# Feed-forward layer after attention: the maximum between the taps, VectorE's results in a PSUM bank, the second norm over slots a group ahead, and w2 loaded in parts

## The chip, the cores and the metric

The program runs on the 8 cores of one Trainium2 chip. Each core takes one sequence of 2048 tokens of width 1024 and works alone; nothing is exchanged. The metric is the device time of the slowest core, in microseconds. The engines are named as in the profile: PE (TensorE), DVE (VectorE), ACT (ScalarE), POOL (GpSimd) and SP (SyncE, which here only starts transfers).

## The reference, cut to what matters

```python
x = x + attention(layernorm(x))            # 16 heads of 64, causal
x = x + ffn(layernorm(x))

def ffn(x):                                # w1 [4096,1024], w2 [1024,4096]
    h = bit_linear(x, w1)                  # x rounded to 8 bits per token, w to -1, 0, 1
    h = depthwise_conv1d(h over tokens, conv_w [4096,1,3], padding 1) + conv_b
    h = silu(h)
    return bit_linear(h, w2)               # h rounded with max|h| over the token's 4096 channels

def act_quant(x):
    scale = 127 / clip(max(|x|, last axis), 1e-5)
    return clip(round(x * scale), -128, 127) / scale
```

The second rounding needs, for each token, the largest absolute value over all 4096 hidden channels. That maximum ("the maximum" below) is what ties the two products together.

## The kernel before, in words

The first half is attention: eight head pairs of 40 slots each (`hp`, `s`), a program order written out by hand for every engine. In the last head pair DVE also takes the statistics of the second norm for the first token tiles, rounds the last pieces of the weights (`weight_step`) and ends with `normalize_ctx`. The sum x1 is spilled to HBM (`x1scr`), and its SBUF space is reused by the feed-forward's buffers, `w2T` among them.

The feed-forward works on 8 groups `G` of 256 tokens. A group has 8 slots `b`, one for each 512 hidden channels (a "quad" `q = 8*G + b`). In every slot:

- PE: `first(q)` makes four blocks `psM[0..3]` of 128 channels by 258 tokens, 8 matmuls each. A block can be overwritten once ACT has read it (`a_tB`) and DVE has read it (`v_tap`). From G = 2 on `second(G-2, b)` follows, 16 matmuls of 512 columns of the second product.
- ACT: `taps(q)` reads each of the four blocks twice, for the right tap with the bias (into `hs`) and the left tap (into `tb`); then `silu(q-1)`, for which POOL must have added `tb` to `hs`.
- DVE: `taps(q)` adds the middle tap from each of the four blocks; `widen_max(q-1)` takes the maximum over the 4 x 128 channels of the quad before, out of what `silu` wrote: a reduction of 128 x 1024 and, but for a group's first quad, a `tensor_tensor` that joins it with the running maximum `amf`.
- POOL: `add_taps(q)`, four additions, then for the group before `scale_h`, four multiplications per quad by the token's scale.

For the group before, DVE rounds the scaled quads into `hqa` or `hqb` (`round_h`, by the table `ROUNDED`; POOL's quads by `SCALED`); `hs` is a ring of 12 quads, so ACT's `taps(q)` waits until quad q-12 is rounded. `token_scale`, `turn_max` and `spread_scale` turn the maximum into the scale row `srow`. `add_out` finishes a half of 128 output rows.

The second norm of the tokens of the next group but one runs beside it: DVE takes `stats` of two token tiles in slots b = 0 and 1 of group G, `spread` and `factors` follow in b = 1 and 2, ACT's `rstd2` (Ln, Exp) in b = 2 and `round_xq` in b = 3 and 4, POOL's `place_xqs`, PE's `transpose_xq` and ACT's `place_xqT` after that. ACT keeps one function table at a time; Ln and Exp, and then Silu, load one each.

SP's queue is in order too. The weight blocks of the first product (`load_w1(q)`, 512 KB) are loaded two slots ahead; the whole of w2 (4 x 1 MB) is loaded in one go in G = 0, b = 5.

Of the kernel before, what the change touches and what calls it, by code (L numbers as in the profile page):

```python
# [16 lines left out]
D = 1024  # L17
# [10 lines left out]
NP = 8  # L28
# [25 lines left out]
def build_program():  # L54
# [23 lines left out]
    with es:  # L78
# [20 lines left out]
        d_x1t = [sem("d_x1t0"), sem("d_x1t1"), sem("d_x1t2")]  # L99
# [133 lines left out]
        x1t = sb("x1t", [128, 3 * D], F32, esB)  # L233
        amx = sb("amx", [128, GRP], F32, esB)
# [4 lines left out]
        psTb = ps("psTb", [128, 1024], BF16, esB)  # L239
        psNb = ps("psNb", [128, 512], F32, esB)  # L240
        psM = [ps(f"psM{i}", [128, 512], F32, esB) for i in range(4)]
# [51 lines left out]
        def tokens(e, st):  # L293
            if st < 5:
                e.wait_ge(g_x1, 4 * (NP - 1) + st // 4 + 1)
                return x1_tile(st)
            e.wait_ge(d_x1t[st % 3], 16 * ((st - 5) // 3 + 1))
            return x1t[:, (st % 3) * D:(st % 3 + 1) * D]

        def lcol(i, k, n):  # L300

            at = 48 * (i % 2) + 3 * k
            return lnc[:, at:at + n]

# [14 lines left out]
        ROUNDED = {3: (0, 1), 4: (2,), 5: (3, 4), 6: (5,), 7: (6,)}  # L319

# [15 lines left out]
        def _(e):  # L336
# [71 lines left out]
            def load_x1t(st):  # L408
                if st >= 8:
                    e.wait_ge(a_xqf, st - 2)  # L410
                e.dma_start(out=x1t[:, (st % 3) * D:(st % 3 + 1) * D],
                            in_=x1scr[128 * st:128 * (st + 1), :]
                            ).then_inc(d_x1t[st % 3], 16)
# [16 lines left out]
            for st in (5, 6, 7):  # L430
                load_x1t(st)
# [3 lines left out]
            for G in range(NGRP + 2):  # L435
                for b in range(8):
                    q = 8 * G + b + 2
                    if 3 <= q < 8 * NGRP:
                        load_w1(q)
                    if b == 1 and G >= 3:  # L440
# [7 lines left out]
                    if b in (6, 7) and 8 <= 2 * G + b - 1 < NT:  # L448
                        load_x1t(2 * G + b - 1)
# [13 lines left out]
        def _(e):  # L463
# [158 lines left out]
            for G in range(NGRP + 1):  # L622
                for b in range(8):
                    if G < NGRP:
                        add_taps(8 * G + b)
                    if b == 4 and G < 7:
                        place_xqs(2 * G + 3)
                    if b == 5 and G < 6:
# [6 lines left out]
        def _(e):  # L635
# [129 lines left out]
            def transpose_xq(st):  # L765
                e.wait_ge(g_xqs, st + 1)
                if st == 0:
# [100 lines left out]
            def turn_max(g):  # L868
                at = (g % 2) * GRP
                e.wait_ge(v_max, 8 * (g + 1))  # L870
                if g >= 1:
                    e.wait_ge(a_srow, g)
                e.transpose(psNb[:, 0:128], amf[:, at:at + 128], idf[:])
# [652 lines left out]
```

## Time and profile before

| what | value |
|---|---|
| time, median of 3 runs | 1073.35 us (1069.76 to 1102.9) |
| time of the profiled execution | 1075.98 us |
| its span on the slowest core (core 6) | 1074.4 us |
| spans of the other cores | 1056.5 to 1072.5 us |
| busy share of the span | PE 83%, DVE 75%, ACT 65%, POOL 64% |
| first matmul of the feed-forward | 522.11 us |
| DMA, mean over the span | 155 GB/s |

The profile is of one execution on one core. A busy share is an average over stages with different limits, so each stage is read for itself.

### The profile page before, as it was taken

How to read it: one execution, taken by the hardware profiler on the slowest of the kernel's cores; microseconds unless marked ns; L12 is line 12 of the kernel's file. 1: busy time of each engine (PE TensorE's matmuls, PEld its weight loads, DVE VectorE, ACT ScalarE, POOL GpSimd, SP SyncE). 2: the span in 40 equal slices, each digit the busy share in tenths (PEclk: the TensorE clock that was granted, in tenths of full speed). 3: DMA queues.
4: the chain of work that ended last, by engine and by line, in shares of the span. 5: the costliest groups of instructions: out<-in, count | busy, mean ns of one | idle time of the engine just before them, and what ended most of it. 6: DMA issues, size and time to landing. Idle time of an engine off the chain costs nothing.

```text
span 1074.4 us, 23923 instructions; the slowest of 8 cores (1056.5 to 1074.4 us)
## 1 busy us (share of the span) xinstructions
PE 895.0 (83%) x7282; PEld 539.3 (50%) x7340; DVE 806.9 (75%) x1293; ACT 698.2 (65%) x1116; POOL 682.7 (64%) x912
## 2 busy tenths in 40 slices
PE   2999989897957778866676578999989899999898
PEld 1454545454524444433554455666656565666443
DVE  2674776777778888977377979898897989888631
ACT  3553888797827676868686866767677676766200
POOL 2211755646655768565454795959879597979590
PEclk9999999999979999967888989999999999999899
DMA  8910777666665766684744221423314233332112
GB/s 265 328 62 1 197 209 236 244 201 223 206 211 173 217 196 202 211 296 161 261 172 182 71 87 59 158 99 132 125 66 151 99 121 116 116 105 96 40 41 77
DMA packets 38749, 166.89 MB, mean 155 GB/s; under 512 B 4833, under 2 KB 4962, under 8 KB 29922
## 3 DMA queue, kind: packets, MB, share of 16 engines
q1 hardware_dynamic: 34210, 148.59, 41.8%
q0 software_dynamic: 4416, 16.78, 4.4%
q8 instruction: 63, 1.03, 0.4%
q14 instruction: 60, 0.49, 0.1%
HBM read 140.18 MB, written 25.17 MB: 154 GB/s over the span
## 4 chain that ended last, share of the span: by engine, by line
PE 42%; DVE 19%; issue 12%; POOL 9%; ACT 8%; DMA 7%; DVEq 1%; SPq 1%; POOLq 0%; ACTq 0%
PE psM L843 9%; PE psO L861 9%; POOL hs L618 6%; PE psQK L680 6%; PE psV L660 5%; PE psS L738 5%; PE psPV L757 5%; DVE hs L1367 3%; ACT PT L999 3%; DVE t1s L1208 3%; DVE amx L1386 3%; ACT hs L1044 2%; DMA wvst<-wv 2%; DMA t1scr<-t8s 2%; ACT tb L1048 2%
## 5 line engine op out<-in xcount | busy, mean ns | idle before, releaser
L999 ACT ACTIVATE PT<-psS,nbias 128x1024 bf16<-128x1024 f32 (+1 forms) x320 | 297.5, 985 | 89.2 <-PE psS L738 85.5
L843 PE MATMUL psM<-xqT,w1b 128*128 128x258 bf16 x2048 | 249.7, 283 | 44.3 <-DVE hs L1367 35.6
L609 POOL TENSOR_TENSOR hs<-hs,tb 128x256 f32<-128x256 f32 x256 | 200.1, 811 | 106.7 <-DVE hs L1367 106.1
L843 PEld LDWEIGHTS psM<-xqT,w1b 128*128 128x128 fp8e4 x2048 | 203.9, 101 | 91.5 <-issue 54.1
L1044 ACT ACTIVATE hs<-psM,convb_s,convw_s 128x256 f32<-128x256 f32 x256 | 146.3, 572 | 99.5 <-PE psM L843 88.0
L618 POOL TENSOR_TENSOR hs<-hs,srow 128x256 f32<-128x256 f32 x256 | 190.0, 775 | 12.0 <-ACT srow L1062 12.0
L680 PE MATMUL psQK<-ln1T,wqkb 128*128 128x512 bf16 x430 | 116.6, 391 | 23.3 <-DVE qkO L1135 7.4
L757 PE MATMUL psPV<-vaug,PT 128*128 128x65 bf16 x2176 | 116.9, 200 | 19.7 <-DVE ctx L1189 10.7
L757 PEld LDWEIGHTS psPV<-vaug,PT 128*128 128x128 bf16 x2176 | 93.1, 101 | 80.1 <-issue 59.4
L1367 DVE SCALAR_TENSOR_TENSOR hs<-psM,convw_s,hs 128x256 f32<-128x256 f32 x256 | 108.5, 473 | 20.1 <-ACT tb L1048 19.4
L1048 ACT ACTIVATE tb<-psM,convw_s 128x256 f32<-128x256 f32 x256 | 121.7, 475 | 0.0
L494 POOL TENSOR_TENSOR PT<-PT,mask_s 128x256 bf16<-128x256 bf16 x128 | 94.0, 750 | 40.9 <-ACT PT L999 39.3
L861 PE MATMUL psO<-w2T,hqa 128*128 128x512 fp8e4 x512 | 117.3, 385 | 0.0
L861 PE MATMUL psO<-w2T,hqb 128*128 128x512 fp8e4 x512 | 114.7, 379 | 2.4 <-DVE hqb L1419 1.7
L1386 DVE TENSOR_REDUCE amx<-hs 128x256 f32<-128x1024 f32 x56 | 108.4, 1936 | 4.6 <-ACT hs L1055 4.6
L505 POOL TENSOR_TENSOR x<-x,ctx 128x128 f32<-128x128 f32 x128 | 70.3, 581 | 56.7 <-DVE ctx L1189 56.5
L861 PEld LDWEIGHTS psO<-w2T,hqa 128*128 128x128 f16 x512 | 50.7, 99 | 57.2 <-issue 3.2
L485 POOL TENSOR_TENSOR sqb<-qkE 128x512 bf16<-128x512 bf16 x32 | 36.6, 1143 | 67.2 <-DVE qkE L1135 64.9
L861 PEld LDWEIGHTS psO<-w2T,hqb 128*128 128x128 f16 x512 | 49.9, 98 | 58.6 <-issue 3.3
L738 PE MATMUL psS<-qkO 64*128 64x512 bf16 (+3 forms) x320 | 62.4, 388 | 19.0 <-ACT PT L999 18.2
L1199 DVE TENSOR_REDUCE smalls<-wbuf 128x1 f32<-128x2048 f32 x32 | 72.8, 2274 | 4.9 <-DMA wbuf<-w2p 3.1
L1055 ACT ACTIVATE hs<-hs 128x1024 f32<-128x1024 f32 x64 | 68.2, 1066 | 12.3 <-POOL hs L609 12.3
(125 smaller groups left out, 1132.8 us busy)
## 6 DMA issues: line engine op xcount, KB each, us to landing
wbuf<-w1q SPq DMA_DIRECT2D x32, 1024.0 KB, 6.4
wbuf<-w2p SPq DMA_DIRECT2D x32, 1024.0 KB, 5.9
w1b<-t1scr SPq DMA_DIRECT2D x64, 512.0 KB, 3.5
x<-x SPq DMA_DIRECT2D x16, 512.0 KB, 15.0
wqkst<-wqk POOLq DMA_DIRECT2D x16, 512.0 KB, 6.7
x1scr<-x POOLq DMA_DIRECT2D x4, 2048.0 KB, 10.1
x1g<-x1scr SPq DMA_DIRECT2D x16, 512.0 KB, 4.4
out<-x1g SPq DMA_DIRECT2D x16, 512.0 KB, 2.6
```

Source lines behind the costliest of these rows:

```text
L609: e.tensor_tensor(hs_quad(q)[:, part], hs_quad(q)[:, part], tb_quad(q)[:, part], ALU.add).then_inc(g_add, 1)
L618: inst = e.tensor_tensor(part, part, srow[:, at:at + GRP], ALU.mult)
L680: inst = e.matmul(bank[:], wqkb[:, at:at + 128], ln1T[:, x0:x0 + 512], start=(kc == 0), stop=(kc == 7))
L738: inst = e.matmul(bP[:, 512 * h + 128 * j:512 * (h + 1)], qk[64 * h:64 * (h + 1), k0:k0 + 128], qk[64 * h:64 * (h + 1), q0:q0 + n], start= ...
L757: inst = e.matmul(psPV[:, 512 * h + VW * m:512 * h + VW * (m + 1)], pt_unit(u)[:, p0:p0 + 128], vaug[:, v0:v0 + VW], start=(kc == 0 and m ...
L843: inst = e.matmul(psM[j][:, 0:GRP + 2], w1b[:, at:at + 128], xqT[:, x0:x0 + GRP + 2], start=(kc == 0), stop=(kc == 7))
L861: inst = e.matmul(psO[n][:], hq_of(g)[:, at:at + 128], w2T[:, D * kc + 512 * n: D * kc + 512 * (n + 1)], start=(kc == 0), stop=(kc == 31))
L999: e.activation(out=pt_unit(u).rearrange("p (h w) -> p h w", w=512)[:, :, 128 * j:512], in_=psS[u % 2][:].rearrange("p (h w) -> p h w", w=512)[
L1044: e.activation(out=hs_quad(q)[:, GRP * j:GRP * (j + 1)], in_=psM[j][:, 2:GRP + 2], func=AF.Identity, scale=convw[:, 3 * hh + 2:3 * hh + 3] ...
L1048: e.activation(out=tb_quad(q)[:, GRP * j:GRP * (j + 1)], in_=psM[j][:, 0:GRP], func=AF.Identity, scale=convw[:, 3 * hh:3 * hh + 1]).then_i ...
L1367: e.scalar_tensor_tensor(sl, psM[j][:, 1:GRP + 1], convw[:, 3 * hh + 1:3 * hh + 2], sl, ALU.mult, ALU.add).then_inc(v_tap, 1)
L1386: done(e.tensor_reduce(amx[:], rows, AX.X, ALU.max, apply_absolute_value=True))
```

## The change

The order of work in the feed-forward is rewritten in these places:

- The maximum of the quad before stands between the second and the third middle tap of a slot, and all else of DVE's slot behind the fourth.
- A PSUM bank, free since `psTb` and `psNb` share one, becomes `psD`. It holds the first part of the maximum, a copy of the identity, and most short results of the second norm and the token scale.
- The statistics of a token tile are split (`moments2`, `largest`, `smallest`) and spread over the slots b = 4 to 7 of the group before and b = 0 and 1; those of batch 1 (tiles 3 and 4) move into the last head pair, slots 29 to 36, with `rstd2(1)` on ACT in slot 33. In G = 0 `round_xq` and what follows come two slots earlier (`TAKEN`).
- w2 is loaded in four parts, one behind each `load_w1` of q = 5 to 8. A fourth buffer for x1 tiles is added.

```diff
-            def taps(q):
-                for j in range(4):
+            def taps(q, js):
+                for j in js:
...
-                    done(e.tensor_reduce(amx[:], rows, AX.X, ALU.max,
+                    done(e.tensor_reduce(psD[:, 0:GRP], rows, AX.X, ALU.max,
                                          apply_absolute_value=True))
                     settled()
-                    e.tensor_tensor(top, top, amx[:], ALU.max
+                    e.tensor_tensor(top, psD[:, 0:GRP], top, ALU.max
                                     ).then_inc(v_max, 1)
...
             for G in range(NGRP + 2):
                 for b in range(8):
                     if G < NGRP:
-                        taps(8 * G + b)
+                        taps(8 * G + b, (0, 1))
+                    if 1 <= 8 * G + b <= 8 * NGRP:
+                        widen_max(8 * G + b - 1)
+                    if G < NGRP:
+                        taps(8 * G + b, (2, 3))
                     if b == 0 and 2 <= G <= NGRP + 1:
                         round_h(8 * (G - 2) + 7)
-                    if 1 <= G <= NGRP:
-                        for k in ROUNDED.get(b, ()):
-                            round_h(8 * (G - 1) + k)
+                    if b == 1 and 1 <= G <= NGRP:
+                        token_scale(G - 1)
                     if b == 0 and G >= 3:
                         add_out(4 * (G - 3) + 3)
                     if b in (2, 4, 6) and G >= 2:
                         add_out(4 * (G - 2) + b // 2 - 1)
-                    if 1 <= 8 * G + b <= 8 * NGRP:
-                        widen_max(8 * G + b - 1)
...
+                    if G < 6:
+
+                        if b == 4:
+                            moments2(G + 2, 0)
+                        if b == 5:
+                            largest(G + 2, 0)
+                        if b == 6:
+                            smallest(G + 2, 0)
+                        if b == 7 and G < 5:
+                            moments2(G + 2, 1)
...
+                    if 1 <= G <= NGRP:
+                        for k in ROUNDED.get(b, ()):
+                            round_h(8 * (G - 1) + k)
...
+                    if s == 33:
+                        rstd2(1)
...
-                    if b == 2 and G < 7:
+                    if b == 1 and 1 <= G < 7:
                         rstd2(G + 1)
...
+                    if s in (29, 31):
+                        moments2(1, (s - 29) // 2)
+                        largest(1, (s - 29) // 2)
+                        smallest(1, (s - 29) // 2)
+                    if s == 31:
+                        variance(1)
+                    if s == 36:
+                        factors(1)
...
+                    if 3 <= q - 2 <= 6:
+                        load_w2(q - 5)
...
-                    if G == 0 and b == 5:
-
-                        e.wait_ge(a_xqf, 5)
-                        for q4 in range(4):
-                            e.dma_start(
-                                out=w2T[:, 8 * q4 * D:8 * (q4 + 1) * D],
-                                in_=t2scr[:, 8 * q4 * D:8 * (q4 + 1) * D]
-                            ).then_inc(d_w2, 16)
```

DVE, group 1, the slots b = 3 and the start of b = 4, with what each row waits for (`hs<-psM` are middle taps, the reduction and the TENSOR_TENSOR behind it the maximum of the quad before, `hqb<-hs` the rounding). Before:

```order
L1367 SCALAR_TENSOR_TENSOR hs<-psM,convw_s,hs 128x256 [waits a_tB] x4
L1419 TENSOR_SCALAR hqb<-hs 128x1024 [waits g_mul] x2
L1386 TENSOR_REDUCE amx<-hs 128x256 [waits a_silu,v_max]
L1389 TENSOR_TENSOR amf<-amf,amx 128x256 [waits v_own]
L1367 SCALAR_TENSOR_TENSOR hs<-psM,convw_s,hs 128x256 [waits a_tB] x4
```

The same place now:

```order
L1410 SCALAR_TENSOR_TENSOR hs<-psM,convw_s,hs 128x256 [waits a_tB] x2
L1429 TENSOR_REDUCE psD<-hs 128x256 [waits a_silu,v_max]
L1432 TENSOR_TENSOR amf<-psD,amf 128x256 [waits v_own]
L1410 SCALAR_TENSOR_TENSOR hs<-psM,convw_s,hs 128x256 [waits a_tB] x2
L1463 TENSOR_SCALAR hqb<-hs 128x1024 [waits g_mul] x2
L1410 SCALAR_TENSOR_TENSOR hs<-psM,convw_s,hs 128x256 [waits a_tB] x2
```

The wait for `a_silu` stood behind all four taps and the two roundings; now it stands ahead of the third tap, and the roundings stand behind the maximum.

DVE, the end of the last head pair (`t1s` and `t8s` are the last weight step, `recb` and `ctx` the last `normalize_ctx`). Before:

```order
L1208 TENSOR_SCALAR t1s<-wbuf,smalls 128x2048
L1211 TENSOR_SCALAR t1s<-t1s 128x2048
L1214 TENSOR_SCALAR t8s<-t1s 128x2048
L1181 RECIPROCAL recb<-psPV 128x8
L1189 TENSOR_TENSOR ctx<-psPV,recb 128x4x64 x2
```

Now, ahead of the same step and behind it (the second tile's statistics and the first of the factors; the first tile's stand above):

```order
L1267 BN_STATS bn6b<-x 128x6
L1268 BN_STATS bn6b<-x 128x6
L1271 BN_AGGR lnc<-bn6b 128x2
L1275 TENSOR_REDUCE psD<-x 128x1
L1280 TENSOR_REDUCE psD<-x 128x1
L1296 TENSOR_SCALAR lnc<-lnc 128x2
L1231 TENSOR_SCALAR t1s<-wbuf,smalls 128x2048
L1234 TENSOR_SCALAR t1s<-t1s 128x2048
L1237 TENSOR_SCALAR t8s<-t1s 128x2048
L1303 TENSOR_TENSOR psD<-psD,lnc 128x2
```

The statistics of two tiles come ahead of the last weight step and the factors between it and `normalize_ctx`.

SP, the loads of G = 0. Before:

```order
L411 DMA x1t<-x1scr 128x1024 x3
L418 DMA x1g<-x1scr 128x1024 x2
L387 DMA w1b<-t1scr 128x4096 x5
L454 DMA w2T<-t2scr 128x8192 x4
L387 DMA w1b<-t1scr 128x4096 x10
```

Now:

```order
L400 DMA w1b<-t1scr 128x4096 x3
L432 DMA w2T<-t2scr 128x8192
L400 DMA w1b<-t1scr 128x4096
L432 DMA w2T<-t2scr 128x8192
L400 DMA w1b<-t1scr 128x4096
L432 DMA w2T<-t2scr 128x8192
L400 DMA w1b<-t1scr 128x4096
L432 DMA w2T<-t2scr 128x8192
L400 DMA w1b<-t1scr 128x4096 x7
```

The block of four parts ahead of the load for q = 8 is taken apart, one part behind each of four blocks of w1.

## Rows read from the trace of the kernel before

**Rows 1.** Busy time by stretch, from one group's last silu to the next

```profile
core 6: us, PE busy (x) PEld busy (x) DVE busy (x) ACT busy (x) POOL busy (x), PEclk, DMA share, GB/s
533.68:579.32 45.64, 32.90 (x250) 25.91 (x249) 33.84 (x60) 37.80 (x71) 23.30 (x33) 0.85 0.53 202
579.32:639.25 59.93, 36.93 (x274) 28.49 (x273) 51.41 (x79) 43.35 (x83) 46.45 (x61) 0.86 0.24 80
639.25:702.79 63.54, 58.39 (x406) 38.34 (x404) 56.30 (x87) 43.66 (x82) 51.71 (x68) 1.00 0.30 100
...
830.31:893.33 63.02, 58.50 (x406) 38.40 (x404) 55.63 (x87) 43.66 (x82) 50.68 (x67) 1.00 0.32 110
893.33:952.31 58.98, 57.41 (x397) 38.25 (x396) 53.27 (x86) 41.39 (x80) 51.00 (x68) 1.00 0.31 108
952.31:1005.23 52.92, 52.92 (x358) 34.83 (x356) 44.39 (x63) 32.94 (x67) 47.04 (x63) 1.00 0.26 91
```

**Rows 2.** Timeline, ACT and DVE in quad 5's slot: start, duration, what, idle before

```profile
559.93 0.64 ACT L1044 ACTIVATE hs<-psM,convb_s,convw_s 128x256 f32<-128x256 f32 x1
...
560.74 1.14 ACT L1055 ACTIVATE hs<-hs 128x1024 f32<-128x1024 f32 x1
...
562.05 1.96 DVE L1386 TENSOR_REDUCE amx<-hs 128x256 f32<-128x1024 f32 x1 [0.53 <-ACT hs L1055]
564.11 0.43 DVE L1389 TENSOR_TENSOR amf<-amf,amx 128x256 f32<-128x256 f32 x1
564.45 1.40 DVE L1367 SCALAR_TENSOR_TENSOR hs<-psM,convw_s,hs 128x256 f32<-128x256 f32 x3
```

**Rows 3.** Timeline, PE and ACT: from a tap to matmuls, from matmuls to ACT

```profile
565.08 3.68 PE L843 MATMUL psM<-xqT,w1b 128*128 128x258 bf16 x32 [0.32 <-DVE hs L1367]
...
596.27 3.68 PE L843 MATMUL psM<-xqT,w1b 128*128 128x258 bf16 x32 [3.12 <-DVE hs L1367]
...
597.41 0.56 ACT L1044 ACTIVATE hs<-psM,convb_s,convw_s 128x256 f32<-128x256 f32 x1 [0.24 <-PE psM L843]
...
600.05 0.56 ACT L1044 ACTIVATE hs<-psM,convb_s,convw_s 128x256 f32<-128x256 f32 x1
```

**Rows 4.** Source lines L1389 and L1367: duration ns min/median/max

```profile
L1389 DVE TENSOR_TENSOR amf<-amf,amx x56: 424/822/996, 544.5 to 1011.8; 128x256 f32<-128x256 f32 x56
...
L1367 DVE SCALAR_TENSOR_TENSOR hs<-psM,convw_s,hs x256: 465/472/485, 525.1 to 1002.0; 128x256 f32<-128x256 f32 x128
```

**Rows 5.** Timeline: PE after an idle stretch in group 1

```profile
587.05 5.67 PE L843 MATMUL psM<-xqT,w1b 128*128 128x258 bf16 x32 [3.49 <-DVE hs L1367]
```

**Rows 6.** Busy time and granted clock of that stretch, columns as in rows 1

```profile
587.00:590.00 3.00, 2.95 (x14) 2.09 (x15) 3.00 (x5) 0.93 (x2) 2.78 (x4) 0.50 0.02 5
```

**Rows 7.** Timeline, ACT: a table load ahead of silu

```profile
790.86 1.28 ACT L1055 ACT_TABLE_LOAD   x1
```

**Rows 8.** Timeline, slot b = 4 of group 4: roundings, and ACT waiting for them

```profile
796.21 2.21 DVE L1419 TENSOR_SCALAR hqb<-hs 128x1024 f16<-128x1024 f32 x2
...
797.49 0.56 ACT L1044 ACTIVATE hs<-psM,convb_s,convw_s 128x256 f32<-128x256 f32 x1 [1.32 <-DVE hqb L1419]
```

**Rows 9.** Timeline, POOL around two scaled quads (b = 4 and 5)

```profile
805.16 1.19 POOL L524 TENSOR_SCALAR xqs<-xqf,lnc 128x1024 bf16<-128x1024 f16 x1
...
812.43 3.23 POOL L609 TENSOR_TENSOR hs<-hs,tb 128x256 f32<-128x256 f32 x4
```

**Rows 10.** Timeline, PE's wait for the last maximum

```profile
1012.51 0.45 PE L873 MATMUL psNb<-idf_s,amf 128*128 128x128 f32 x1 [4.74 <-DVE amf L1389]
```

**Rows 11.** Timeline, PE at the first slot of group 1

```profile
573.05 8.87 PE L843 MATMUL psM<-xqT,w1b 128*128 128x258 bf16 x64 [4.29 <-DMA w1b<-t1scr]
```

**Rows 12.** Timeline, DVE at the end of attention: two tiles' statistics, the last wait

```profile
477.19 0.69 DVE L1246 BATCH_NORM_STATS2 bn6b<-x 128x6 f32<-128x512 f32 x1 [1.33 <-POOL x L505]
...
480.77 0.68 DVE L1246 BATCH_NORM_STATS2 bn6b<-x 128x6 f32<-128x512 f32 x1
...
518.01 0.21 DVE L1181 RECIPROCAL recb<-psPV 128x8 f32<-128x8 f32 x1 [8.79 <-PE psPV L757]
```

More of the change, by code:

```diff
@@ L98, in build_program @@
         d_w1 = [sem("d_w1_0"), sem("d_w1_1"), sem("d_w1_2")]
-        d_x1t = [sem("d_x1t0"), sem("d_x1t1"), sem("d_x1t2")]
+        d_x1t = [sem(f"d_x1t{i}") for i in range(4)]
         d_x1g = [sem("d_x1g0"), sem("d_x1g1")]
@@ L408, in load_x1t, with load_w2 @@
             def load_x1t(st):
[L409 to L411 removed]
+                if st >= 9:
+                    e.wait_ge(a_xqf, st - 3)
+                e.dma_start(out=x1t[:, (st % 4) * D:(st % 4 + 1) * D],
                             in_=x1scr[128 * st:128 * (st + 1), :]
[L413 removed]
+                            ).then_inc(d_x1t[st % 4], 16)
+            def load_w2(q4):
+                if q4 == 0:
+                    e.wait_ge(a_xqf, 5)
+                e.dma_start(out=w2T[:, 8 * q4 * D:8 * (q4 + 1) * D],
+                            in_=t2scr[:, 8 * q4 * D:8 * (q4 + 1) * D]
+                            ).then_inc(d_w2, 16)
             def load_x1g(u):
@@ L429, in _ @@
             e.wait_ge(d_x1s[1], 16)
-            for st in (5, 6, 7):
+            e.wait_ge(d_x1s[2], 16)
+            for st in range(5, 9):
                 load_x1t(st)
@@ L1262, in var_of, with variance @@
                     "p (n k) -> p n k", k=2)[:, :, 1]
-            def spread(i):
+            def variance(i):
                 n = len(batch(i))
@@ L1280, in factors @@
                 settled()
+                e.tensor_tensor(pcol(i, 12, n), pcol(i, 2, n), mean_of(i, n),
+                                ALU.subtract)
+                done(e.tensor_tensor(lcol(i, 13, n), pcol(i, 3, n),
+                                     mean_of(i, n), ALU.add))
+                settled()
+                done(e.tensor_tensor(pcol(i, 7, n), pcol(i, 12, n),
+                                     lcol(i, 13, n), ALU.max))
+                settled()
                 e.wait_ge(a_rstd2, i + 1)
-                done(e.tensor_tensor(lcol(i, 14, n), lcol(i, 7, n),
+                done(e.tensor_tensor(pcol(i, 14, n), pcol(i, 7, n),
@@ L1345, in _ @@
                     place_bias(c - 1)
-                if hp == NP - 1 and s in (9, 12, 16):
-                    stats(0, s // 4 - 2)
-                if hp == NP - 1 and s == 16:
-                    spread(0)
-                if hp == NP - 1 and s == 21:
-                    factors(0)
+                if hp == NP - 1:
+                    if s in (12, 14, 17):
+                        moments2(0, (12, 14, 17).index(s))
+                        largest(0, (12, 14, 17).index(s))
+                        smallest(0, (12, 14, 17).index(s))
+                    if s == 17:
+                        variance(0)
+                    if s == 21:
+                        factors(0)
+                    if s in (29, 31):
[6 more added lines that the diff above has]
+                        factors(1)
                 if slot in STEPS:
@@ L1432, in add_out @@
                                        ALU.mult, ALU.add).then_inc(v_epi2, 1)
+            done(e.tensor_copy(psD[:, 256:384], idf[:]))
+            settled()
             for G in range(NGRP + 2):
```

117 lines of the change are left out of this document (62 added, 55 removed).

## The prediction

> **What bounds the kernel now.** I read the busy time by stretch first, cut at the start of each group's last silu, since silu is where the hidden quads pass from one engine to the next. The feed-forward has three regimes [rows 1]. In the first two stretches (groups 0 and 1, 45.64 and 59.93 us) PE runs only the first product: it is busy 33 and 37 us, at a granted clock of 0.85, and ACT, DVE and POOL set the pace. The next four, of which the first and the last are shown, take 254.1 us together, 63.5 each: PE is busy for 58.4, DVE for 56.3, POOL for 51.7. The sixth takes 58.98, and in the seventh (52.92, seven slots and a short one) PE is busy all the time. PE needs about 7.0 us a slot when nothing holds it. So there are some 5 us to win in each of four groups, more in groups 0 and 1, and nothing in the last. A slot of DVE is so full before because the statistics sit in b = 0 and 1.
>
> Then I looked for who waits for whom within a slot: timelines of the slots where an engine stands idle and the releaser is named [rows 2, 3]. A small latency means nothing in a sum of busy times, but it counts where the order closes a ring.
>
> **The ring that the change closes.** Before, DVE took all four taps of quad q and then the maximum of q-1; a late silu was worth a slot of slack. Now the third and the fourth tap stand behind the maximum of q-1, and that waits for silu(q-1), which ACT runs behind its own taps of q. The third tap frees `psM[2]`, PE can then make block 2 of q+1, ACT must read blocks 2 and 3, and only then comes silu(q). One turn advances by exactly one slot, and it has no slack in it. Its length, step by step:
> - silu starts to reduction starts: 562.05 - 560.74 = 1.31 us; reduction to the joining TENSOR_TENSOR: 564.11 - 562.05 = 2.06 [rows 2].
> - TENSOR_TENSOR to tap: 564.45 - 564.11 = 0.34 [rows 2]. The new one reads one operand from PSUM, as the tap does; so it should take the tap's 0.47, not 0.43, and the step 0.38.
> - tap to matmuls: 565.08 - 564.45 = 0.63 [rows 2, 3].
> - matmuls to ACT's read: 597.41 - 596.27 = 1.14; one block on ACT: (600.05 - 597.41) / 3 = 0.88 [rows 3].
> - the last block's read to silu: 560.74 - 559.93 = 0.81 [rows 2].
>
> The sum is 7.21 us a slot. That is a floor for every slot that has taps, whatever is taken off DVE's load. It is just above PE's 7.0, so it costs little where PE was the bound, but where PE has only the first product a slot could be shorter than that.
>
> **What lies on the ring beside it**, in each of groups 1 to 6:
> - The table load ahead of silu, 1.28 us [rows 7], once a group, since Ln and Exp stand between two silus. 1.3. The one ahead of Ln fits into ACT's wait for PE, as do `round_xq` and `place_xqT`.
> - The roundings. In b = 3 they now come behind the maximum and the fourth tap, and ACT's taps of b = 4 need the first of them (ring of 12 quads). Counted from silu: 3.75 to the third tap, two taps of 0.46 (three take 1.40) [rows 2], and ACT starts 797.49 - 796.21 = 1.28 after the first rounding [rows 8]: 5.95. Four blocks and silu follow, 3 x 0.88 + 0.81, which makes 9.40 against 7.21: 2.2.
> - POOL in b = 4. It can add blocks 2 and 3 only behind the late taps: 4.22 + two additions of 0.81 = 5.9. Then `place_xqs` and two scaled quads, 812.43 - 805.16 = 7.3, and four additions of the next quad, 3.23 [rows 9]: done at 16.4, where silu is due at 14.4. 2.0.
> - 0.5 for PE's transposes and POOL's next slot, an estimate from the same rows.
>
> Together 6.0, so a group takes 8 x 7.21 + 6.0 = 63.7. Against the stretches [rows 1]:
> - group 0: 7 x 7.21 = 50.5 against 45.64: +4.8. Here the statistics are gone, the batch 1 table loads too, and it is still longer.
> - group 1: 63.7 against 59.93: +3.8.
> - four groups: 254.8 against 254.1: +0.7.
> - the sixth stretch: 63.7 against 58.98: +4.7.
> - the seventh: seven slots, 5.6 us to the last silu (it follows the two late taps and POOL's two additions, with no taps of ACT ahead), the roundings' 2.2 and POOL's 0.8 (no `place_xqs` there): 59.1 against 52.92: +6.2.
>
> That is +20.2.
>
> **PE's clock in groups 0 and 1.** There PE has 3.7 us of work a slot, so in a turn of 7.2 it stands idle for 3.5 us, and what it does next is the ring's own step. After 3.12 us idle the trace has four blocks in 3.68 us [rows 3]; after 3.49 us in 5.67 us, at a granted clock of 0.50, the 1.2 GHz level [rows 5, 6]. [...] The two blocks in the ring at half clock cost 1.8 us more; the whole difference of these rows is 2.0. Over 15 slots that is 27, less some 4 in group 1, where PE is waited for less because the roundings and POOL are late: 23. Idle stretches will not all be equal, the first two blocks of the next quad may come apart from the others, and neighbouring rows lie on both sides: I take two thirds, +16, and keep 0 and 23 as ends. The Trainium skill (TensorE: Matmul & The Clock Gate, section on HAM oscillation) describes this for another kernel: idle gaps between bursts of matmuls put every burst that follows at half clock, not some of them. By it all 15 slots would pay, which is a rival below.
>
> **The other parts.**
> - Results in PSUM. The joining TENSOR_TENSOR takes 0.42 us at best and 0.82 in the median [rows 4], the tap with one operand in PSUM never over 0.49. So about 0.35 goes in seven of eight slots, 2.5 us a group of DVE's time, and some of the tiny operations of the norm with it. All of it falls into DVE's wait for silu, so I cost it at nothing. If the new form still took 0.82, the ring would be 0.35 longer, some 17 us over 49 slots; if PE rather than the ring bounds, it is a gain (the rival).
> - DVE's other work has 7.21 less the maximum and the taps, 7.21 - 2.44 - 1.84 = 2.9 us a slot; DVE's 56.3 us a group [rows 1] less eight taps and maxima leave about 2.4. It fits, if spread; a slot that overflows lengthens the ring directly, 0 to 1 us a group.
> - w2 in parts. PE waited 4.29 us for the block of w1 behind it [rows 11]. With one 1 MB part ahead of each block and two slots of 7.2 us in hand it is hidden; were it not, at most these 4.3 us come back. The gain lies inside group 0, which the ring already gives a length.
> - End of attention. Two tiles' statistics, 480.77 - 477.19 = 3.6 us each, go ahead of the last weight step and the factors behind it. DVE then waited 8.79 us for PE [rows 12], which hides them. ACT gets `rstd2(1)` with a wait for DVE in the middle of its exponents: +1.2, between 0.5 and 3. Behind DVE's later last step stands SP's last store of w2, and the feed-forward's start behind that; if the cover is too short it costs up to 2 more.
> - The tail. The last maximum no longer waits for POOL and a rounding: 1.31 + 2.06 + 0.6 = 4.0 after the last silu (1005.23 [rows 1]) in place of 1012.51 - 1005.23 = 7.3 [rows 10]: -3.3. POOL's scaling of the last group follows from that directly.
>
> **The sum.** 20.2 + 16 + 1.2 - 3.3 = +34 us on the profiled execution's 1075.98 (span 1074.4). That execution lies 2.6 over the median of three, so I put the difference on the median: 1073.35 + 34 = 1107 us.
>
> **The rivals.**
> 1. Clock low in every slot of groups 0 and 1 (the page's rule, above): +23 instead of +16, 1114 us, up to 1122 with the upper ends of the small terms. For it: rows 5. Against it: the 3.12 us idle that stayed fast.
> 2. The ring binds, PE stays at full clock: 20.2 + 1.2 - 3.3 = +18, 1091 us; 1080 if the roundings and POOL also cost half. For it: rows 3, and the 3.5 us are near that row too.
> 3. The change does nothing to speak of: what the ring costs in groups 0, 6 and 7 comes back from DVE's lighter load, because DVE's wait for a full slot was longer than I see. 1073, between 1063 and 1080.
> 4. Faster: the ring does not bind, DVE's load does. Then the four groups come down to the 59.0 of the sixth stretch (-18), group 0 to ACT's 37.8 busy (-7.8), group 1 to DVE's 51.4 (-8.5) [rows 1], and the tail gives 3.3: -36, 1037 us. It decides from a turn of under 7.0 us. Against it: every step is a measured start to start, and the smallest alternative rows shorten it by 0.2 at most. For it: in four long stretches DVE and PE both are near full, and that is what spreading the statistics helps.
>
> **Chances.** Forecast (1098 to 1112) 0.40, rival 1 0.14, rival 2 0.24, rival 3 0.10, rival 4 0.12. A measurement of this kernel tells 2% from no change, so slower begins at 1095: the forecast, rival 1 and the upper fifth of rival 2 give 0.58; rival 3, the rest of rival 2 and a little of rival 4 within 2%, 0.31; faster 0.11. The range leaves out rival 4 and the top of rival 1: 1066 to 1122 us.
>
> **What would show it.** In the new profile: silus 7.2 us apart in the second half with DVE idle ahead of each reduction, released by silu, and PE idle ahead of its first-product matmuls, released by the tap; groups 0 and 1 at 50 to 75 us each with a granted clock near 0.75; the TENSOR_TENSOR at 0.47; the table load only in ACT's rows of b = 1; no wait for a transfer at the start of group 1; the last maximum 4 us behind the last silu. I am wrong if DVE has no idle time ahead of the maximum, or silus in group 0 lie closer than 7 us.

## The result, and the profile after

The changed kernel takes 1100.88 us (median of 5 runs, 1098.02 to 1141.68) against 1073.35: a ratio of 1.025, 95% interval 1.021 to 1.029. The top of the range is a run in which half of the cores ran at a lower clock, and every ratio here leaves such runs out. It is slower by 27.5 us, and the forecast was 1107, 34 slower. The profiled execution has a span of 1096.4 us on its slowest core (core 3) against 1074.4 (core 6), 22.0 more.

Busy time by stretch of the changed kernel, cut at each group's last silu as in [rows 1]; the sixth and seventh stretch stand fourth and fifth here, and the last row runs to the end of the program:

```profile
528.30:583.94 55.64, 34.30 (x230) 25.21 (x231) 32.11 (x49) 35.34 (x67) 21.63 (x30) 0.80 0.53 191
583.94:647.42 63.48, 39.68 (x278) 29.09 (x277) 48.62 (x82) 43.23 (x83) 46.71 (x63) 0.86 0.24 84
...
712.63:775.61 62.98, 58.34 (x406) 38.33 (x405) 52.41 (x89) 43.63 (x83) 50.06 (x67) 1.00 0.35 118
...
903.80:971.72 67.92, 60.78 (x398) 39.02 (x397) 49.57 (x78) 41.55 (x80) 48.09 (x66) 0.95 0.29 94
971.72:1031.25 59.53, 56.12 (x368) 35.42 (x366) 43.06 (x63) 33.06 (x67) 46.91 (x64) 1.00 0.24 81
1031.25:1096.40 65.15, 54.62 (x244) 24.27 (x244) 18.84 (x26) 1.44 (x2) 27.65 (x36) 0.97 0.17 65
```

Against [rows 1]: group 0 +10.0, group 1 +3.6, the four middle stretches +2.3 together (65.21, 62.98, 65.21, 62.98), the sixth +8.9, the seventh +6.6, the stretch behind the last silu -4.0 (65.15, against 1074.4 - 1005.23 = 69.17). Silu 0 came 5.4 us earlier, at 528.30 against 533.68. That adds up to the 22.0 us between the spans.

One core of one execution has its own accidents, so here is the same division for all eight cores of the two profiled executions (us, changed less before):

| stretch | forecast | slowest cores | mean of eight cores |
|---|---|---|---|
| up to silu 0 | +1.2 | -5.4 | +0.9 |
| group 0 | +4.8 | +10.0 | +9.0 |
| group 1 | +3.8 | +3.6 | +5.0 |
| PE's clock in groups 0 and 1 | +16 | in the two rows above | in the two rows above |
| four middle stretches | +0.7 | +2.3 | +2.9 |
| sixth | +4.7 | +8.9 | +5.1 |
| seventh | +6.2 | +6.6 | +6.7 |
| behind the last silu | -3.3 | -4.0 | -3.5 |
| together | +34 | +22.0 | +26.3 |

The point to see is DVE: in the four middle stretches it is busy for 53.4 us in the mean in place of 56.1, 2.7 us less, and the stretches are no shorter (64.1 us for 63.5). Work went away and waiting took its place.

Who waits, in the feed-forward of the changed kernel (us in total, times, longest):

```profile
ACT hs L1067 <- PE psM L862: 113.8, 72, 3.5
DVE psD L1429 <- ACT hs L1078: 88.9, 44, 4.7
...
PE psM L862 <- DVE hs L1410: 68.5, 44, 4.2
...
ACT hs L1067 <- DVE hqb L1463: 15.5, 3, 7.9
ACT hs L1078 <- POOL hs L625: 14.4, 7, 5.2
ACT hs L1067 <- DVE hqa L1463: 12.4, 3, 4.8
...
PE psM L862 <- DMA w1b<-t1scr: 3.0, 1, 3.0
```

The first three close a circle: DVE's maximum waits for silu, PE's first product for DVE's tap, ACT's read for PE. In the kernel before, PE waited 35.6 us for the tap and the reduction 4.6 us for silu. One turn of that circle, timeline of quads 27 and 28:

```profile
744.85 1.10 ACT L1078 ACTIVATE hs<-hs 128x1024 f32<-128x1024 f32 x1
...
746.11 1.95 DVE L1429 TENSOR_REDUCE psD<-hs 128x256 f32<-128x1024 f32 x1 [2.17 <-ACT hs L1078]
...
748.17 0.42 DVE L1432 TENSOR_TENSOR amf<-psD,amf 128x256 f32<-128x256 f32 x1
...
748.51 0.87 DVE L1410 SCALAR_TENSOR_TENSOR hs<-psM,convw_s,hs 128x256 f32<-128x256 f32 x2
...
749.13 1.92 PE L862 MATMUL psM<-xqT,w1b 128*128 128x258 bf16 x16 [1.75 <-DVE hs L1410]
...
750.27 0.56 ACT L1067 ACTIVATE hs<-psM,convb_s,convw_s 128x256 f32<-128x256 f32 x1 [1.56 <-PE psM L862]
...
751.15 0.57 ACT L1067 ACTIVATE hs<-psM,convb_s,convw_s 128x256 f32<-128x256 f32 x1
...
751.97 1.05 ACT L1078 ACTIVATE hs<-hs 128x1024 f32<-128x1024 f32 x1
```

The steps are 1.26, 2.06, 0.34, 0.62, 1.14, 0.88 and 0.82: 7.12 us. From silu to silu the undisturbed slots of the whole second half take 7.06 to 7.13 us. Each middle group has three longer ones: 8.61 with the table load, 9.47 where ACT waits for the roundings (798.35 to 807.82, and alike in other groups), and 9.45 where POOL is late.

One thing the prediction did not have. Timeline of DVE, POOL and ACT in group 6 of the changed kernel:

```profile
930.64 2.77 POOL L625 TENSOR_TENSOR hs<-hs,tb 128x256 f32<-128x256 f32 x4
...
931.47 5.83 DVE L1463 TENSOR_SCALAR hqb<-hs 128x1024 f16<-128x1024 f32 x2
...
933.37 2.77 POOL L634 TENSOR_TENSOR hs<-hs,srow 128x256 f32<-128x256 f32 x4
...
936.90 0.56 ACT L1067 ACTIVATE hs<-psM,convb_s,convw_s 128x256 f32<-128x256 f32 x1 [7.91 <-DVE hqb L1463]
```

Two roundings, 2.2 us together in [rows 8], take 5.83 here: the first stands open over POOL's eight operations in a row, which end at 936.14. ACT, which needs the buffer, loses 4 us more than in other groups (a slot of 13.6 us). On core 0 of the same execution this slot is 9.5 us, so it is a matter of how the engines happen to lie to one another.

### The profile page after: what moved, and what is told of

Read it like the earlier page. It is cut to its first block, busy times and chain, and to the rows that moved or that the text cites. A ratio compares the mean times of both kernels' runs of the same rounds, so it can differ in the third digit from the quotient of the medians.

```text
span 1096.4 us, 24048 instructions; the slowest of 8 cores (1083.4 to 1096.4 us)
## 1 busy us (share of the span) xinstructions
PE 913.0 (83%) x7340; PEld 539.9 (49%) x7340; DVE 783.5 (71%) x1302; ACT 695.9 (63%) x1114; POOL 677.8 (62%) x912
## 4 chain that ended last, share of the span: by engine, by line
PE 45%; DVE 15%; issue 11%; POOL 11%; ACT 10%; DMA 6%; DVEq 1%; SPq 0%; POOLq 0%; ACTq 0%
PE psM L862 11%; PE psO L880 9%; PE psQK L696 7%; DVE psD L1429 5%; PE psV L676 5%; PE psS L754 5%; PE psPV L773 5%; POOL hs L634 5%; ACT hs L1078 3%; ACT PT L1020 3%; DVE hs L1410 2%; POOL hs L625 2%; ACT tb L1071 2%; DMA wvst<-wv 2%; DMA x1scr<-x 2%
## 5 line engine op out<-in xcount | busy, mean ns | idle before, releaser
L862 PE MATMUL psM<-xqT,w1b 128*128 128x258 bf16 x2048 | 260.1, 285 | 75.8 <-DVE hs L1410 68.5
L625 POOL TENSOR_TENSOR hs<-hs,tb 128x256 f32<-128x256 f32 x256 | 195.4, 786 | 146.4 <-DVE hs L1410 139.2
L634 POOL TENSOR_TENSOR hs<-hs,srow 128x256 f32<-128x256 f32 x256 | 186.3, 759 | 8.2 <-ACT srow L1085 8.2
L1429 DVE TENSOR_REDUCE psD<-hs 128x256 f32<-128x1024 f32 x56 | 108.7, 1941 | 89.2 <-ACT hs L1078 88.9
L696 PE MATMUL psQK<-ln1T,wqkb 128*128 128x512 bf16 x480 | 130.1, 397 | 6.7 <-DVE qkO L1158 5.2
L1410 DVE SCALAR_TENSOR_TENSOR hs<-psM,convw_s,hs 128x256 f32<-128x256 f32 x256 | 112.0, 475 | 12.1 <-ACT tb L1071 11.5
L521 POOL TENSOR_TENSOR x<-x,ctx 128x128 f32<-128x128 f32 x128 | 73.8, 607 | 57.7 <-DVE ctx L1212 57.5
L1078 ACT ACTIVATE hs<-hs 128x1024 f32<-128x1024 f32 x64 | 67.8, 1059 | 14.6 <-POOL hs L625 14.4
```

Source lines behind the costliest of these rows:

```text
L625: e.tensor_tensor(hs_quad(q)[:, part], hs_quad(q)[:, part], tb_quad(q)[:, part], ALU.add).then_inc(g_add, 1)
L634: inst = e.tensor_tensor(part, part, srow[:, at:at + GRP], ALU.mult)
L696: inst = e.matmul(bank[:], wqkb[:, at:at + 128], ln1T[:, x0:x0 + 512], start=(kc == 0), stop=(kc == 7))
L862: inst = e.matmul(psM[j][:, 0:GRP + 2], w1b[:, at:at + 128], xqT[:, x0:x0 + GRP + 2], start=(kc == 0), stop=(kc == 7))
L1410: e.scalar_tensor_tensor(sl, psM[j][:, 1:GRP + 1], convw[:, 3 * hh + 1:3 * hh + 2], sl, ALU.mult, ALU.add).then_inc(v_tap, 1)
L1429: done(e.tensor_reduce(psD[:, 0:GRP], rows, AX.X, ALU.max, apply_absolute_value=True))
```

## The experiments

All are timed against the kernel before on the same chip; "us" below is the median of all runs. A bracket is the 95% interval of the ratio to the kernel before.

**Where the maximum stands.** Three kernels differ from the changed one only in the two calls of `taps` around `widen_max`:

```diff
-                        taps(8 * G + b, (0, 1))
+                        taps(8 * G + b, (0, 1, 2, 3))   # or (0, 1, 2), or (0,)
                     if 1 <= 8 * G + b <= 8 * NGRP:
                         widen_max(8 * G + b - 1)
                     if G < NGRP:
-                        taps(8 * G + b, (2, 3))
+                        taps(8 * G + b, ())             # or (3,), or (1, 2, 3)
```

> The changed kernel with one edit: the maximum of the quad before stands behind all four taps instead of between the second and the third; everything else of the change stays. Ring theory (the turn silu, maximum, third tap, matmuls, ACT's reads, next silu sets 7.07 us for every slot): the ring has two slots a turn now, so silus come 7.0 apart or closer, the slots of b=3 lose the 2.4 us of the late rounding and those of b=4 the 2.4 us of POOL's late additions; groups 2 to 5 take 57 to 60 us instead of 63 to 65, group 0 some 42 instead of 55, and the time falls to 1035 to 1055 us. Rival (the loss comes from the other parts: results in PSUM, statistics at the end of attention, the clock): 1090 us or more.

> The changed kernel with the maximum between the third and the fourth tap, so that only block 3 of the four is freed behind it. Ring theory: the turn loses one block on ACT, 7.07 - 0.88 = 6.2 us; under PE's 7.0 in groups 2 to 7, above ACT's own pace in group 0. Groups 2 to 5 about 59 to 61 us, group 0 about 45 to 50, time 1050 to 1075 us. Rival: no change against 1101, since the place of the maximum is not the cause.

> The changed kernel with the maximum between the first and the second tap: three blocks are freed behind it. Ring theory: the turn gains one block on ACT, 7.07 + 0.88 = 7.95 us, in each of 63 slots: silus 7.95 apart, + 45 to 60 us, 1145 to 1160 us, less where other waits are absorbed. Rival: the same 1101 us.

Measured: behind all four taps 1041.09 us, 0.969 [0.967, 0.972]; between the third and the fourth 1072.99, 0.999 [0.996, 1.001]; behind the first 1154.07, 1.075 [1.072, 1.079]. The undisturbed slots, those with no further wait, are 6.2 to 6.3 us with the maximum ahead of the fourth tap, 7.1 ahead of the third, and 7.9 to 8.0 ahead of the second. The step is 0.88, which is one block of ACT: each tap that comes behind the maximum puts one more block on the ring between PE's matmuls and the next silu. With the maximum last the ring is open. The same view of that kernel:

```profile
531.69:577.62 45.93, 27.54 (x219) 21.87 (x217) 31.25 (x44) 34.76 (x68) 19.54 (x27) 0.85 0.69 236
577.62:633.18 55.56, 37.90 (x286) 29.28 (x287) 48.59 (x83) 42.87 (x82) 45.78 (x63) 0.91 0.29 99
...
748.28:805.80 57.52, 57.52 (x406) 38.84 (x405) 52.17 (x89) 43.34 (x82) 49.21 (x67) 1.00 0.37 120
```

PE is busy for all of the 57.5 us of this middle group, so in it no other engine holds PE up. So the rest of the change is worth 32 us, and the maximum's place takes 60 back.

**The maximum's place alone**, put into the kernel before, with nothing else of the change:

```diff
-                        taps(8 * G + b)
+                        taps(8 * G + b, (0, 1))
+                    if 1 <= 8 * G + b <= 8 * NGRP:
+                        widen_max(8 * G + b - 1)
+                    if G < NGRP:
+                        taps(8 * G + b, (2, 3))
```

> The kernel before with this one edit: the maximum between the second and the third tap; statistics, SBUF results and the load of w2 as before. Ring theory: 7.1 us a slot at least here too, with the joining operation at up to 0.8 us inside the ring (7.5) and the statistics of b=0 and 1 not hidden: slower than the changed kernel or equal, 1100 to 1125 us. Rival (the other parts cost): 1070 to 1078 us, as before.

Measured: 1123.87 us, 1.045 [1.041, 1.049]. One part alone costs 50 us. The undisturbed slot is again 7.1, in kernels with different loads of DVE. A middle group is 68.5 us, 5.5 above the changed kernel's 63.0. Of this, 4.2 fall on the two slots at the start of a group (19.9 us in place of 15.7), where DVE's whole statistics now stand ahead of the taps; the other 1.3 are 0.2 to 0.4 in each of four slots, which fits the results in SBUF.

**VectorE's own results back in SBUF**, in the changed kernel and in the one with the maximum last:

```diff
-        psD = ps("psD", [128, 512], F32, esB)
+        psD = sb("psD", [128, 512], F32, esB)
```

> The changed kernel with VectorE's own results (psD) in SBUF again, nothing else. The joining operation then takes 0.82 us in the median, as in the kernel before, in place of 0.42, and it stands in the ring. If the ring sets every slot of the first product, seven slots of eight grow by 0.4 us, 7.1 to 7.5 us from silu to silu, and the whole by 56 x 0.4 = 22 us less what the waits for POOL and the roundings absorb: 1116 to 1123 us against 1101. The prediction's price of nothing (it falls into VectorE's wait for silu) gives 1101 us and slots of 7.1 us.

> The changed kernel with the maximum behind all four taps (1041 us), and psD in SBUF. Here the joining operation is on no ring, PE is busy all the time in four groups (57.3 of 57.3 us) and VectorE has 5 us of idle time a group. Theory: 2.5 to 3 us more of VectorE's work a group fall into that idle time; 1041 to 1046 us. Rival, VectorE's load sets the group as soon as it is not spread evenly over the slots: 2.5 us in each of seven groups, 1058 us.

Measured: 1115.49 us, 1.039 [1.036, 1.041], 14.6 above the changed kernel, and 1052.83 us, 0.980 [0.977, 0.982], 11.7 above the kernel with the maximum last. The first comes near my theory's size, the second lies between the theory and its rival, and in both the price is mostly not where I had looked. With the ring, a group goes from 63.0 to 66.5 us: two slots are 7.5 in place of 7.1, which is the joining operation, and the one behind `factors` is 12.0 in place of 9.5. I had expected 0.4 in seven slots of eight, but in this kernel the joining operation, although in SBUF, has a median of 0.426 us: it is slow (0.64 to 1.03) in 18 of 56 cases only. DVE in the chain of the slot behind `factors`, first with SBUF, then as changed:

```profile
746.22 0.59 DVE L1315 TENSOR_SCALAR psD<-psD 128x2 f32<-128x2 f32 x1
...
746.99 0.50 DVE L1318 TENSOR_SCALAR psD<-psD,smalls 128x2 f32<-128x2 f32 x1
747.59 0.58 DVE L1322 COPY lnc<-psD 128x2 f32<-128x2 f32 x1
```

```profile
797.27 0.17 DVE L1315 TENSOR_SCALAR psD<-psD 128x2 f32<-128x2 f32 x1
...
797.63 0.21 DVE L1318 TENSOR_SCALAR psD<-psD,smalls 128x2 f32<-128x2 f32 x1
797.94 0.16 DVE L1322 COPY lnc<-psD 128x2 f32<-128x2 f32 x1
```

Two elements a partition take 0.5 to 0.6 us there, while POOL works through its additions, and 0.16 to 0.21 with the input in PSUM. Summed over the twelve operations of `factors` (means of their lines), that is 4.95 us against 2.50 in a group, and they stand ahead of the taps and the roundings of b = 3, for which ACT waits. With the maximum last the same slot goes from 8.9 to 11.6 us; there the twelve operations explain 1.9 of the 2.7 (3.93 us against 2.01 in that group; 1.6 in the mean of six groups), and the rest I have not split. The Trainium skill (SBUF — State Buffer, section "Who interferes with whom") says that an instruction of VectorE with two inputs in SBUF, or in a two-port mode, contends with GpSimd, and one with at most one such input outside these modes does not. The rows agree, and the one operation of `factors` that still has both inputs in SBUF in the changed kernel shows it too: `L1327` takes 0.71 us in the median there. Not each operation pays, though: with everything in SBUF four of the twelve (`L1305`, `L1317`, `L1323`, `L1327`) still take 0.15 to 0.17 us in the first four of six groups, and why these go free no run here shows.

**Roundings ahead of the maximum**, which is the order of the kernel before, in the changed kernel and in the one with the maximum last:

```diff
                         taps(8 * G + b, (0, 1))
+                    if 1 <= G <= NGRP:
+                        for k in ROUNDED.get(b, ()):
+                            round_h(8 * (G - 1) + k)
                     if 1 <= 8 * G + b <= 8 * NGRP:
...
-                    if 1 <= G <= NGRP:
-                        for k in ROUNDED.get(b, ()):
-                            round_h(8 * (G - 1) + k)
```

> The changed kernel with each slot's roundings between the first two taps and the maximum, in place of last in the slot. VectorE waits there for silu, 2.0 us in the mean, and one rounding takes 0.7 to 1.2 us. Theory: the slots behind b = 3 come down from 9.5 to the ring's 7.1 or to 7.5 (two roundings of up to 2.3 us do not quite fit), and so do the late slots of 8.9 to 13.6 us in which ACT waited for a rounding that stood behind the maximum: 2.4 us in seven groups, and 5 to 10 us more in all: 1074 to 1084 us. Rival: POOL's late slot (b = 4) takes the place of the wait that goes, since both lie in neighbouring slots: 1095 to 1101 us.

> The changed kernel with the order taps, roundings, maximum: no ring, and roundings ahead of the maximum. Theory: with PE busy all the time in the middle groups (57.3 us) there is nothing to win there; in groups 1 and 7, and where ACT waited for a rounding (21 us in 5 waits, most of them hidden behind PE's buffers), 0 to 6 us: 1035 to 1041 us. Rival: the roundings now delay the maximum and with it POOL's work on the last group, or share the port with POOL's additions: 1041 to 1050 us.

Measured: 1161.90 us, 1.082 [1.080, 1.085], in the changed kernel; 1040.21 us, 0.968 [0.965, 0.971], with the maximum last. The second is as expected, no gain where PE is the bound. The first refutes both my theory and its rival: 60 us lost where I expected 20 won. The timeline shows a second ring:

```profile
764.18 1.65 DVE L1410 SCALAR_TENSOR_TENSOR hs<-psM,convw_s,hs 128x256 f32<-128x256 f32 x4
...
764.86 1.41 POOL L625 TENSOR_TENSOR hs<-hs,tb 128x256 f32<-128x256 f32 x2 [2.35 <-DVE hs L1410]
766.22 2.77 POOL L634 TENSOR_TENSOR hs<-hs,srow 128x256 f32<-128x256 f32 x4
...
769.17 1.06 DVE L1463 TENSOR_SCALAR hqa<-hs 128x1024 f16<-128x1024 f32 x1 [3.34 <-POOL hs L634]
770.33 1.95 DVE L1429 TENSOR_REDUCE psD<-hs 128x256 f32<-128x1024 f32 x1
...
772.72 0.87 DVE L1410 SCALAR_TENSOR_TENSOR hs<-psM,convw_s,hs 128x256 f32<-128x256 f32 x2
```

Late taps, POOL's additions behind them, POOL's scaled quad behind those, DVE's rounding behind that, then the maximum and the late taps again. DVE waits 127 us for `L634` in that run, 17 in the changed kernel. Slots of 12.8 to 14.4 us come twice a middle group. This second ring is read from the rows; no run opens it while it keeps the first. I had counted only how long a rounding takes, not for whom it waits.

**The load of w2 as one block** of 4 MB at b = 5 of group 0, with the maximum last:

> The version with the maximum behind all four taps (1041 us) and the load of w2 as one block of 4 MB at b = 5 of group 0, as in the kernel before. Theory: PE waits again for the block of w1 behind it at the turn to group 1, 4.3 us there in the kernel before, and since slots of this version are shorter (5.8 us in the mean of group 0, 7.2 with the ring) up to 6 us: 1043 to 1047 us. Rival, the transfer is hidden behind the two blocks of w1 in hand: 1041 us.

```diff
-                    if 3 <= q - 2 <= 6:
-                        load_w2(q - 5)
...
+                    if G == 0 and b == 5:
+                        for q4 in range(4):
+                            load_w2(q4)
```

Measured: 1044.88 us, 0.971 [0.967, 0.974]. The interval contains that of the load in parts, so the two can't be told apart, and the medians are 3.8 us apart. The profiles speak for the rival: with the block no core waits for a w1 load at the turn to group 1. The one such wait of a core (6.7 to 9.4 us) comes early in group 0, as with the load in parts (7.2 to 11.2), and group 0 is no longer (49.6 us from silu 0 to silu 8 in the mean of the cores, 49.9 in parts).

**SyncE's wait for the last spilled quarter of x1, moved** behind the first loads of w1, with the maximum last and with the roundings ahead of it:

```diff
             load_x1g(1)
-            x1_spilled(e)
...
                     if 3 <= q - 2 <= 6:
+                        if q == 5:
+                            x1_spilled(e)
                         load_w2(q - 5)
```

> The same version (1041 us), with SyncE's wait for the last spilled quarter of x1 moved from before its first load of w1 in the feed-forward to before the first part of w2. In the profile of this version PE waits once 11.2 us for that load, in the slot behind quad 1. Theory: the load then starts as soon as quad 1 has left its buffer and the wait goes nearly whole, though ACT, DVE and POOL have 0 to 3 us of their own left there: 1030 to 1036 us. Rival, the load is slow as it runs beside the spill and the loads of x1, or VectorE's wait for the same spill at its first rounding takes over: 1038 to 1041 us.

> The version with taps, roundings, maximum in each slot (1040 us), and SyncE's wait moved as in the run before this one. Theory: the two are independent, so it stands where that run stands, 1029 to 1036 us. Rival: 1038 to 1041 us.

Measured: 1042.16 us, 0.968 [0.964, 0.973], and 1035.15 us, 0.964 [0.962, 0.967]. PE's longest wait for w1 fell from 11.2 us to 7.3 in the first, from 9.2 to 7.0 in the second, and did not go. That is on the slowest cores; over all cores it was 7.2 to 11.2 before the first move and up to 9.6 behind it, and 7.0 to 9.8 before the second and 6.4 to 9.7 behind it. The first shows no gain, the second is 5 us better than its like with intervals that just overlap. So the wait for the spill was at most a small part of that load's lateness; what holds the rest stays open. The second is the fastest kernel of this study, 39 us under the kernel before.

**The statistics bunched** in b = 0 and 1 of a group, as before, with the maximum last:

```diff
-                    if b == 1 and 1 <= G < 7:
+                    if b == 2 and 1 <= G < 7:
                         rstd2(G + 1)
...
-                        if b == 4:
-                            moments2(G + 2, 0)
...
+                        if b == 0 or (b == 1 and G < 6):
+                            moments2(G + 1, b)
+                            largest(G + 1, b)
+                            smallest(G + 1, b)
+                        if b == 1:
+                            variance(G + 1)
```

> The version with the maximum behind all four taps (1041 us), with the statistics of a group's two tiles whole in b = 0 and 1 of groups 1 to 6, as in the kernel before, in place of pieces over b = 4 to 1; batch 1 stays at the end of attention. Each of these two slots then has 4 us more of VectorE's work (9.5 to 11 us against PE's 7.0). Theory: that is what held the middle groups at 63.5 us; less the 2.9 us for results in PSUM, they come to 60.5 in place of 57.3: 1060 to 1064 us. Rival, VectorE catches up in the slots that follow and PE stays busy: 1041 to 1045 us.

Measured: 1060.27 us, 0.988 [0.986, 0.990], 19.2 above the kernel with the statistics spread. The total is the theory's, though a middle group takes 62.8 and not 60.5, and PE has idle time in every middle group again:

```profile
758.66:821.80 63.14, 58.53 (x406) 38.48 (x405) 55.00 (x88) 42.98 (x82) 49.06 (x67) 1.00 0.32 109
```

Two slots in each middle group are long, 10.8 and 11.8 us, where they are 6.0 and 8.9 with the statistics spread. DVE's load over the whole group is 55.0 us of 63.1, less than the 57.5 that the group takes with the statistics spread, so it was not the sum that bound but where it stood. The slot ahead of those two is 7.5 in place of 8.6, as the table load moves out of it: with the statistics ACT's `rstd2` goes one slot later too, from b = 1 back to b = 2, and no run tells that part from the rest.

These prices add up, if each holds beside the others. From 1073.4, statistics spread -19.2 and results in PSUM -11.7 give 1042.5, where 1041.1 was measured; what is left is -1.4, the net of w2, of the end of attention, which costs 3, and of the stretch behind the last silu, which gives some 4. Then the maximum between the taps, with its roundings behind it: +59.8, 1100.9.

## Why the prediction was right

- **The ring.** Forecast 7.21 us a turn, measured 7.07 to 7.12. The steps, read from a kernel that did not have the ring, were each right to 0.05. The joining operation took 0.42 and not the 0.47 that I gave it. The three kernels with the maximum elsewhere show it to be the cause, and fix how it grows, by 0.88 a tap.
- **The roundings.** Forecast 9.40 for the slot behind b = 3, measured 9.47. POOL in b = 4 was given 2.0; it costs 2.4. The table load costs 1.5 for 1.3. A group without other trouble takes 63.0, where 63.7 was forecast.
- **The stretches.** In the mean of the eight cores the sixth stretch is +5.1 for +4.7, the seventh +6.7 for +6.2, the stretch behind the last silu -3.5 for -3.3, and the four middle ones +2.9 for +0.7. Groups 0 and 1 are +14.0 together, where +8.6 and the clock's +16 were forecast.
- **Missed: roundings that POOL blocks.** The sixth stretch came out at +8.9 for +4.7, and two of the middle ones 2.2 us long. `L1463` took up to 5.2 us; I had used 1.1 for one [rows 8]. It is some 8 us of the profiled core. Other cores have it too: of the 32 middle stretches of the eight cores 17 are 65.2 to 66.4 us long and have one rounding of 3.3 to 3.7 us each, and the 15 without one are 63.0 to 63.4. That is some 5 us a core. The sixth stretch of core 3, with its rounding of 5.2 us, is the only one of its kind.
- **Too large: PE's clock in groups 0 and 1.** Forecast +16. On the profiled core the slots of group 0 stand 6.2 us above 7 x 7.07, up to 3.0 of it PE's wait for w1, and group 1 is 63.5 us, 0.5 above a middle group that has only the ring, the roundings and POOL. In the mean of the cores it is 5.5 (of it up to 2.9 the wait for w1) and 1.8. So the clock took some 3 to 7 us. PE's matmuls of the first product in the two stretches of the changed kernel:

```profile
528.30:583.94 55.64, 33.21 (x214) 24.00 (x215) 0.80 0.53 191
583.94:647.42 63.48, 36.77 (x252) 26.46 (x250) 0.86 0.24 84
```

  That is 0.155 and 0.146 us each, against 3.68 / 32 = 0.115 at the full clock [rows 3], so by this estimate 35% and 27% of them ran at 1.2 GHz. The term of +16 had two of four blocks slow in two thirds of the slots, a third of the matmuls: the share was about right. The step that failed is the price, that each slot with such blocks grows by 1.8 us. PE's rows of the last three turns of group 0 show this:

```profile
564.96 5.18 PE L862 MATMUL psM<-xqT,w1b 128*128 128x258 bf16 x32 [2.84 <-DVE hs L1410]
573.49 3.83 PE L862 MATMUL psM<-xqT,w1b 128*128 128x258 bf16 x32 [3.35 <-DVE hs L1410]
580.52 5.35 PE L862 MATMUL psM<-xqT,w1b 128*128 128x258 bf16 x32 [3.20 <-DVE hs L1410]
```

  The first burst lost 1.3 us against the middle one, and its slot is 8.53 us, 1.5 above the ring. The last lost 1.5, and its slot is 7.61, 0.5 above: part of the slow blocks lies beside the ring. In group 1 sixteen matmuls take 3.60 us at 608.08, nearly twice 1.92, and the slot, long from other waits, is 8.93 us, where the same slot of a middle group is 9.47. The forecast took 4 us off for this overlap. The rival by which every slot pays (1114 us) falls too: the slot of the middle burst is 7.04 us, another of the group 7.06. Nor does the length of the idle time alone decide: behind 3.35 us the burst is fast, behind 2.84 it is not, and in the kernel before one burst of 32 took 4.98 us behind 3.03 us of idle time, where another took 3.68 behind 3.12 [rows 3]. What decides stays open. Two thirds of 23 are also 15.3, not 16.
- **Mis-sized: the end of attention.** From the normalization at 466.09 to the first matmul of the feed-forward at 517.35 are 51.3 us, where it was 474.11 to 522.11, 48.0. So it took 3.3 and not 1.2, past the 3 that I gave as the upper end, though within it if the 2 us of a cover that is too short are added. Between the last row of that normalization (`nrm<-psN 1x2`) and the first matmul it is 3.2 more in the mean of the eight cores. No run takes the statistics, the factors and `rstd2(1)` there apart. On the profiled core silu 0 came earlier only since what lies ahead of that point was 8 us shorter in this execution; the other kernels' first silus spread from 523.8 to 536.9.
- **Costed at nothing: results in PSUM.** They are worth 14.6 us, with the ring, and I said that all of it falls into DVE's wait. The joining operation has no such wait behind it: where it is slow it lengthens the slot by 0.4, in two slots of eight, and in most others it is at 0.42 in SBUF too. The twelve small operations of `factors` don't fall into that wait either, as they stand ahead of what ACT waits for. This did not spoil the sum, because the group's 63.7 was built up from steps that did not contain them; it would have, had the change left them in SBUF.
- **w2 in parts.** Hidden, as forecast; what remained was a 3.0 us wait at another load.

In the mean of the cores groups 0 and 1 were forecast 10.6 us too long and the rest 2.7 too short, which leaves the 7.8 us between 34.1 and 26.3. So the number is near partly by luck: the clock's term hid what was missing elsewhere, and 1100.9 lies between the forecast and rival 2, 1091, the ring without the clock. The ring, which decides the sign, was read right. What rival 4 gave for a ring that does not bind, 1037 us, is what the maximum behind the taps measured: 1041.

## What to carry to other kernels

Before an instruction that waits for another engine is moved ahead of one that frees a buffer, follow the buffer round: if the way leads back to the waited-for engine within one turn, the sum of that way's start-to-start steps is a floor for the turn, however much work is taken off the engine. Order each engine's queue so that what frees buffers for others comes first and what waits for a result just made comes last, and check for every instruction put ahead of the wait for whom it waits itself. Spreading the same operations evenly over the slots gave 19 us, so look at the fullest slot, not at the busy share of the group.

## What was not expected of the hardware

- Most of DVE's operations on 2 elements a partition with everything in SBUF took 0.50 to 0.67 us while POOL worked, and 0.15 to 0.21 with the input in PSUM. The same line in SBUF goes down to 0.161 us, so waiting and not the size made their time. The joining TENSOR_TENSOR took 0.423 to 0.426 us in all 56 cases with an operand in PSUM, and up to 0.996 before [rows 4]. Duration ns, min/median/max, in the kernel with the results back in SBUF and in the changed one:

```profile
L1308 DVE TENSOR_TENSOR psD<-psD,lnc x8: 161/507/509, 490.4 to 944.7; 128x2 f32<-128x2 f32 x6, 128x3 f32<-128x3 f32 x1, 128x1 f32<-128x1 f32 x1
```

```profile
L1308 DVE TENSOR_TENSOR psD<-psD,lnc x8: 166/168/170, 483.6 to 924.9; 128x2 f32<-128x2 f32 x6, 128x3 f32<-128x3 f32 x1, 128x1 f32<-128x1 f32 x1
```

- A rounding from SBUF to SBUF can stand open through several of POOL's operations in a row, not only one. The longest of these, 5.2 us, is the one above that lay beside eight of them:

```profile
L1463 DVE TENSOR_SCALAR hqb<-hs x32: 681/1090/5225, 675.0 to 1067.2; 128x1024 f16<-128x1024 f32 x32
```

- With the two rings of the roundings-first kernel PE waited up to 7.3 us, and its granted clock fell to 0.93 in the middle groups too, where the changed kernel has 1.00: waiting costs PE a second time.
